# A decoder layer on one NeuronCore: where VectorE leaves the recurrence's state between its scan and the product with C

## The chip, the cores and the metric

One Trainium2 chip, one of its cores (five engines: TensorE or PE, VectorE or DVE, ScalarE or ACT, GpSimd or POOL, and SyncE, which issues the DMAs). The metric is the device time of one execution in microseconds (us); lower is better.

## The reference, cut to what matters

The kernel computes one decoder layer for 64 sequences of 128 tokens with 512 features: a Mamba block, a banded cross attention and a mixture of 8 small experts, each behind a layer norm and added to x. The change is in the Mamba block:

```
proj = einsum('blh,ph->blp', x, in_proj_w);  h_in, gate = split(proj)
u    = silu(conv(h_in) + conv_b)                          # I = 1024 channels
ts, Bm, Cm = split(einsum('bli,pi->blp', uT, x_proj_w))   # N = 16 states
dt   = softplus(einsum('blr,ir->bli', ts, dt_proj_w) + dt_proj_b)
dA   = exp(dt[..., None] * A);   dBx = (dt * uT)[..., None] * Bm[:, :, None, :]
hstates = scan over l of  h = dA * h + dBx
y    = einsum('blin,bln->bli', hstates, Cm) + D * uT
y    = y * silu(gate);   out = einsum('bli,hi->blh', y, out_proj_w)
```

## The kernel before

**Groups.** The 64 sequences go in 32 groups of GB = 2. An iteration g of a software pipeline does the state recurrence of group g ("cur"), the projections, convolution and step sizes of group g + 1 ("nxt"), the output projection and attention of group g - 1 ("p1") and the experts of group g - 2 ("p2"). One iteration from the middle is written twice inside a loop over g; the first three and the last four stand on their own. Every engine has its own list of calls, written out by hand; nothing reorders them, and engines meet through semaphores that count up.

**The 64 steps of a group.** The 1024 channels are 8 blocks `ic` of 128 partitions, the 16 states are 8 pairs `r`; step s = 8 ic + r handles one block and one pair of states: 2 states x 2 sequences x 128 tokens = 512 elements per partition. A step has five parts:

- `decays(g, s)` on ScalarE (lines 452 to 465): two ACTIVATE of 254 elements write exp(delta * a) into PSUM bank s % 2 (`DAR = 2`). Four of the bank's 512 elements, those at token 0 of every state and sequence, are zero and are never written (the memset of line 1392 sets them once), so that the scan starts anew there. It waits for `h_done` of scan s - 2, which read that bank last.
- `times_b(g, s)` on GpSimd (L300): du * B into slot s % 8 of the SBUF ring `ring`. It waits for `hc_used`, which TensorE raises when it has read the slot's last tenant.
- `scan(g, s)` on VectorE (L1454): reads decays from PSUM and the ring slot, writes the states over the ring slot.
- The product with C over the same ring slot: `times_c` on VectorE (L1439) for the 24 steps of `DVE_C` (s % 8 is 1, 4 or 7), on GpSimd (L309) for the other 40. Both read the slot and `bc`, both in SBUF. SyncE may load the next group's `bc` row r once product 56 + r is made.
- `y_sum(g, s)` on TensorE (L1066): transposes of the slots of steps s - 1 and s, added up in PSUM bank 2.

The product and the scan on VectorE as they stand:

```
nc.vector.tensor_tensor(ring[:, s % RING, :], ring[:, s % RING, :],
                        bc[:, s % RS, 2:4, :].rearrange("p a t -> p (a t)"),
                        ALU.mult).then_inc(hcd_done, 1)
nc.vector.tensor_tensor_scan(ring[:, s % RING, :], ps[:, s % DAR, :], ring[:, s % RING, :], 0.0, ...)
```

**What stands between.** VectorE's list also has the softplus (`soft_step`, L1423 to L1434, two SBUF tensors each), the convolution (L1582), the layer norms' statistics, the product with the gate (`y_step`, L1448), the attention's row maxima (L1489), `addq` (L1496), `rden` (L1499), `on` (L1503) and the router. Between `decays`, ScalarE evacuates PSUM banks 3 to 7 for TensorE (copies L526, L551, L561, L566, L596; the attention's exp L592; layer norm L469; step size L489) and loads an activation table (ACT_TABLE_LOAD) when it goes from one function set to another. `attention(.., "wide")` (L600) on ScalarE waits for `rden`, TensorE's L1040 for it, and `on` for that.

## Time and profile before

| | |
|---|---|
| median of 3 runs | 5532.19 us (5530.11 to 5533.7) |
| profiled execution's own time | 5533.42 us |
| its span, first to last instruction | 5531.6 us |
| busy: DVE / PE / POOL / ACT | 90% / 87% / 82% / 73% of the span |
| granted TensorE clock | 0.964 of 2.4 GHz over the span |

Busy is the time in which an engine ran at least one instruction. The idle time of a group of instructions is what the engine stood still just before them, with the instruction that ended it ("releaser"). The chain of waits is followed back from the last instruction: at each step to what released it, or to the instruction before it on its engine; "issue" in it is time in which the engine waited for nothing that the profile shows. Instructions of one engine overlap a little in the timeline: 1.21 us scans follow each other every 1.13 us.

### The profile page before, as it was taken

To read this page: it belongs to the slowest core of one execution; us is meant where nothing else is said; L and a number is where in the kernel's file an instruction comes from. 1 tells how busy PE (TensorE), PEld (TensorE's weight loads), DVE (VectorE), ACT (ScalarE), POOL (GpSimd) and SP (SyncE) were. 2 spreads that over 40 slices of the span, in tenths; PEclk is the share of its full clock that TensorE was granted. 3 is DMA by queue.
4 is the path that set the end of the run, shared out by engine and by line. 5 is a ranking of instruction groups with operands and counts; after the bars stand their busy time and mean duration, and the time that the engine had idled before them with its cause. 6 is when DMAs were issued, how large, how long until landed. Compare 5 with 4: busy or idle time off the path is not lost.

```text
span 5531.6 us, 139169 instructions
## 1 busy us (share of the span) xinstructions
PE 4796.2 (87%) x51012; PEld 3435.7 (62%) x51012; DVE 4955.4 (90%) x7075; ACT 4058.8 (73%) x7812; POOL 4541.5 (82%) x3464
## 2 busy tenths in 40 slices
PE   5788888988888988888989888989888988898876
PEld 3566666666666666666666666666666666666653
DVE  3999999999999999999999999999999999999972
ACT  3677777877777777777877777777777777777752
POOL 2988888888888888888888888888888888888870
PEclk8899999999999999999999999999999999999986
DMA  3211222221212221212221222221212221221100
GB/s 112 71 63 42 70 68 74 70 66 42 74 64 74 70 67 41 74 64 74 71 67 40 74 64 74 74 70 34 77 64 70 74 74 38 70 69 66 62 9 11
DMA packets 114693, 350.19 MB, mean 63 GB/s; under 512 B 13057, under 2 KB 14849, under 8 KB 113921
## 3 DMA queue, kind: packets, MB, share of 16 engines
q1 hardware_dynamic: 114048, 341.51, 19.0%
q8 instruction: 416, 6.82, 0.5%
q14 instruction: 229, 1.87, 0.1%
HBM read 323.64 MB, written 17.83 MB: 62 GB/s over the span
## 4 chain that ended last, share of the span: by engine, by line
PE 46%; DVE 18%; issue 15%; POOL 11%; ACT 7%; DVEq 1%; POOLq 0%; ACTq 0%
POOL ring L300 7%; PE ps L1066 7%; PE ps L1114 6%; DVE ring L1454 5%; PE ps L1096 5%; PE ps L982 4%; PE ps L957 4%; POOL ring L309 4%; PE ps L1134 3%; PE ps L1010 3%; DVE nmax L1489 3%; ACT ps L462 3%; DVE ring L1439 2%; DVE tmp L1423 2%; PE ps L1021 1%
## 5 line engine op out<-in xcount | busy, mean ns | idle before, releaser
L300 POOL TENSOR_TENSOR ring<-du,bc 128x512 f32<-128x512 f32 x2048 | 2741.9, 1356 | 577.7 <-PE ps L1066 352.3
L1454 DVE TENSOR_TENSOR_SCAN ring<-ps,ring 128x512 f32<-128x512 f32 x2048 | 2456.7, 1211 | 201.2 <-POOL ring L300 103.1
L462 ACT ACTIVATE ps<-delta,a_neg 128x254 f32<-128x254 f32 x4096 | 1761.5, 468 | 326.9 <-DVE ring L1454 320.9
L309 POOL TENSOR_TENSOR ring<-ring,bc 128x512 f32<-128x512 f32 x1280 | 1776.5, 1394 | 232.5 <-DVE ring L1454 230.6
L1066 PE MATMUL ps<-ident,ring 128*128 128x128 f32 x8192 | 1103.7, 282 | 73.7 <-DVE ring L1439 43.1
L1066 PEld LDWEIGHTS ps<-ident,ring 128*128 128x128 f32 x8192 | 962.9, 145 | 193.5 <-issue 119.1
L1439 DVE TENSOR_TENSOR ring<-ring,bc 128x512 f32<-128x512 f32 x768 | 755.4, 987 | 3.4
L592 ACT ACTIVATE probs_mem<-ps 128x768 f32<-128x768 f32 (+1 forms) x512 | 455.9, 911 | 176.0 <-PE ps L1010 174.4
L1134 PE MATMUL ps<-w_in,xt_a 128*128 128x256 f32 x2048 | 488.8, 394 | 12.8 <-DVE hc L1582 8.1
L1114 PE MATMUL ps<-xt_a,w_in 128*128 128x256 f32 x2048 | 476.6, 386 | 7.1 <-DVE hc L1582 4.1
L1096 PE MATMUL ps<-w_outp,yz 128*128 128x512 f32 x1024 | 462.5, 599 | 18.7 <-ACT yz L526 18.7
L1489 DVE TENSOR_REDUCE nmax<-ps 128x8 f32<-128x1280 f32 x256 | 380.7, 1487 | 78.4 <-PE ps L982 73.8
L1134 PEld LDWEIGHTS ps<-w_in,xt_a 128*128 128x128 f32 x2048 | 398.1, 200 | 68.4 <-DVE hc L1582 8.9
L1114 PEld LDWEIGHTS ps<-xt_a,w_in 128*128 128x128 f32 x2048 | 381.6, 191 | 76.7 <-issue 17.7
L1582 DVE SCALAR_TENSOR_TENSOR hc<-ps,conv_w,hc 128x254 f32<-128x254 f32 (+2 forms) x768 | 363.1, 473 | 62.2 <-ACT hc L537 42.7
L1096 PEld LDWEIGHTS ps<-w_outp,yz 128*128 128x128 f32 x1024 | 190.1, 191 | 227.9 <-issue 199.8
L982 PE MATMUL ps<-qk 32*32 32x160 f32 (+2 forms) x16384 | 296.2, 297 | 0.0
L1010 PE MATMUL ps<-qk 32*128 32x192 f32 (+1 forms) x4096 | 286.8, 397 | 0.0
L1021 PE MATMUL ps<-probs_mem,v_aug 128*32 128x192 f32 (+1 forms) x4096 | 229.8, 367 | 44.0 <-ACT probs_mem L592 43.9
L579 ACT ACTIVATE qk<-ps,b_qk 128x512 f32<-128x512 f32 x256 | 170.6, 678 | 125.6 <-PE ps L957 125.6
L957 PE MATMUL ps<-xb,w_qk 128*128 128x512 f32 x512 | 241.1, 593 | 2.8 <-ACT qk L579 1.3
L1010 PEld LDWEIGHTS ps<-qk 32*128 32x128 f32 x4096 | 186.3, 197 | 68.4 <-issue 63.1
(136 smaller groups left out, 6362.2 us busy)
## 6 DMA issues: line engine op xcount, KB each, us to landing
w_in<-in_w_in SPq DMA_DIRECT2D x256, 512.0 KB, 3.7
bc<-bc_rows SPq DMA_DIRECT2D x256, 512.0 KB, 4.1
x_new<-in_x SPq DMA_DIRECT2D x32, 512.0 KB, 6.2
x_res<-in_x SPq DMA_DIRECT2D x32, 512.0 KB, 5.5
enc<-in_ctx SPq DMA_DIRECT2D x64, 256.0 KB, 5.3
out<-x_att SPq DMA_DIRECT2D x32, 512.0 KB, 2.8
w_outp<-in_w_outp SPq DMA_DIRECT2D x1, 2048.0 KB, 8.0
bc_rows<-bc_sb SPq DMA_DIRECT2D x32, 32.0 KB, 1.5
```

The lines of the kernel that those rows point to most:

```text
L300: nc.gpsimd.tensor_tensor(ring[:, s % RING, :].rearrange("p (n t) -> p n t", n=2), du[:, q % 2, (ic % 2) * NT:(ic % 2 + 1) * NT].rearrange ...
L309: nc.gpsimd.tensor_tensor(ring[:, s % RING, :], ring[:, s % RING, :], bc[:, s % RS, 2:4, :].rearrange("p a t -> p (a t)"), ALU.mult).then_ ...
L462: nc.scalar.activation(ps[:, s % DAR, (n % 2) * NT:(n % 2 + 1) * NT].rearrange("p (b t) -> p b t", b=GB)[:, :, 1:T], delta[:, ic, :].rearr ...
L982: last = nc.tensor.matmul(ps[32 * a:32 * a + 32, PS_ATT + hp, j * NEAR + lo:j * NEAR + hi], qk[r:r + 32, j, n * P + 32 * a:n * P + 32 * a ...
L1010: last = nc.tensor.matmul(ps[:, PS_ATT + hp, a * WIN + lo:a * WIN + hi], qk[r:r + 32, 2 + j, blk * P:(blk + 1) * P], qk[r:r + 32, j, at:at ...
L1066: last = nc.tensor.matmul(ps[:, PS_Y, b * T:(b + 1) * T], ring[:, t % RING, n * NT + b * T:n * NT + (b + 1) * T], ident[:], start=False, s ...
L1096: last = nc.tensor.matmul(ps[:, PS_ATT + b, :], yz[:, ic, b * T:(b + 1) * T], w_outp[:, ic, :], start=(ic == 0), stop=(ic == NI - 1))
L1114: last = nc.tensor.matmul(ps[:, PS_B, a * NT:(a + 1) * NT], w_in[:, slot, k, a * P:(a + 1) * P], xt_a[:, k, :], start=(k == 0), stop=(k == ...
L1134: last = nc.tensor.matmul(ps[:, PS_B, b * NT:(b + 1) * NT], xt_a[:, k, b * T:(b + 1) * T], w_in[:, slot, k, :], start=(k == 0), stop=(k == ...
L1439: nc.vector.tensor_tensor(ring[:, s % RING, :], ring[:, s % RING, :], bc[:, s % RS, 2:4, :].rearrange("p a t -> p (a t)"), ALU.mult).then_ ...
L1454: nc.vector.tensor_tensor_scan(ring[:, s % RING, :], ps[:, s % DAR, :], ring[:, s % RING, :], 0.0, ALU.mult, ALU.add).then_inc(h_done, 1)
L1489: nc.vector.tensor_reduce(nmax[:, n].rearrange("p j (a r) -> p a j r", r=32)[:, :, :, DH], ps[:, PS_ATT:PS_ATT + 4, 0:NJ * NEAR].rearrange ...
```

## The change

1. For the 24 steps of `DVE_C`, `scan` writes the states over the decays in PSUM bank s % 2, in place of the ring slot. `times_c` on VectorE reads them from there and writes the product to the ring slot.
2. Since the next user of the bank would overwrite states that the product still needs, `decays` of step s + 2 waits for that product (`hcd_done`) where s is in `DVE_C`. The scan has also overwritten the bank's four zeros, so `decays` first copies four zeros from a new SBUF tile `zeros` to their places (one ScalarE COPY of 4 elements).
3. VectorE's list has every `times_c(g, s)` close behind `scan(g, s)` and ahead of `scan(g, s + 2)`. Seventeen of the 24 move forward, product 63 from the next iteration to the end of its own; products 1, 17, 23, 31, 39, 47 and 60 keep their place behind their scan.
4. GpSimd sets `zeros` at the start, and three waits count it.

```diff
@@ decays, ScalarE
+                if (s - DAR) % SG in DVE_C:
+                    reached(act, hcd_done, g * NDC + dvc(s - DAR + 1) if s >= DAR else (g - 1) * NDC + dvc(s - DAR + SG + 1))
+                    nc.scalar.copy(ps[:, s % DAR, :].rearrange("p (k t) -> p k t", t=T)[:, :, 0:1],
+                                   zeros[:].rearrange("p (k o) -> p k o", o=1)).then_inc(da_reset, 1)
                 act.wait_ge(h_done, g * SG + s + 1)
@@ times_c, VectorE
-                nc.vector.tensor_tensor(ring[:, s % RING, :], ring[:, s % RING, :],
+                nc.vector.tensor_tensor(ring[:, s % RING, :], ps[:, s % DAR, :],
@@ scan, VectorE
-                nc.vector.tensor_tensor_scan(ring[:, s % RING, :], ps[:, s % DAR, :], ring[:, s % RING, :], 0.0,
+                state = ps[:, s % DAR, :] if s in DVE_C else ring[:, s % RING, :]
+                nc.vector.tensor_tensor_scan(state, ps[:, s % DAR, :], ring[:, s % RING, :], 0.0,
@@ iteration, VectorE (three of the moves)
                 if cur:
                     scan(g, 36)
+                    times_c(g, 36)
                     scan(g, 37)
...
                     attention(g, 1, "max", 3)
                 if cur:
-                    times_c(g, 36)
                     scan(g, 39)
...
                 if cur:
-                    times_c(g, 55)
                     scan(g, 57)
+                    times_c(g, 57)
                 if p1:
                     attention(g, 1, "rden")
                 if cur:
                     scan(g, 58)
-                    times_c(g, 57)
```

The order of VectorE's instructions late in an iteration, from the layer norm's statistics to `soft_step`, before (scans of 56 and 57 ahead of `rden`, product 55 between them; L1454 is the scan and L1439 the product):

```order
L1408 TENSOR_SCALAR ln_rs_e<-ln_mv_e 128x1
L1438 REGISTER_ALU
L1439 TENSOR_TENSOR ring<-ring,bc 128x512
L1452 REGISTER_ALU
L1454 SCALAR_TENSOR_TENSOR ring<-ps,ring 128x512
L1499 RECIPROCAL rden<-ps 128x32
L1452 ISA
L1454 SCALAR_TENSOR_TENSOR ring<-ps,ring 128x512
L1438 REGISTER_ALU
L1439 TENSOR_TENSOR ring<-ring,bc 128x512
L1503 TENSOR_TENSOR o_sb<-ps,o_sb 128x512 x2
```

Now, the same place (L1463 is the scan, L1447 the product, L1508 `rden`, L1512 `on`):

```order
L1416 TENSOR_SCALAR ln_rs_e<-ln_mv_e 128x1
L1460 REGISTER_ALU
L1463 SCALAR_TENSOR_TENSOR ps<-ps,ring 128x512
L1446 REGISTER_ALU
L1447 TENSOR_TENSOR ring<-ps,bc 128x512
L1508 RECIPROCAL rden<-ps 128x32
L1460 ISA
L1463 SCALAR_TENSOR_TENSOR ring<-ps,ring 128x512
L1512 TENSOR_TENSOR o_sb<-ps,o_sb 128x512 x2
```

Product 57 went from behind scan 58 to ahead of `rden`; product 55 went to behind scan 55.

ScalarE's instructions around the decays of steps 49, 50 and 51, before (the three rows of L462 ACTIVATE; x2 is one step's pair):

```order
L526 COPY yz<-ps 128x256
L462 ACT_TABLE_LOAD
L462 ACTIVATE ps<-delta,a_neg 128x2x127 x2
L460 REGISTER_ALU
L462 ACTIVATE ps<-delta,a_neg 128x2x127 x2
L595 ISA
L596 COPY o_sb<-ps 128x512
```

Now (the decays are L470, the resets L466):

```order
L534 COPY yz<-ps 128x256
L197 REGISTER_ALU
L466 COPY ps<-zeros 128x4
L470 ACT_TABLE_LOAD
L470 ACTIVATE ps<-delta,a_neg 128x2x127 x2
L468 REGISTER_ALU
L470 ACTIVATE ps<-delta,a_neg 128x2x127 x2
L603 ISA
L604 COPY o_sb<-ps 128x512
L197 REGISTER_ALU
L466 COPY ps<-zeros 128x4
```

A reset stands ahead of the decays of step 49 (whose bank step 47 used), and one ahead of those of step 51; the number of table loads is the same.

## Rows read from the trace of the kernel before

**Rows 1.** The page: span, busy time of each engine.
```profile
span 5531.6 us, 139169 instructions
PE 4796.2 (87%) x51012; PEld 3435.7 (62%) x51012; DVE 4955.4 (90%) x7075; ACT 4058.8 (73%) x7812; POOL 4541.5 (82%) x3464
```
**Rows 2.** The chain that ended last, shares by engine.
```profile
PE 46%; DVE 18%; issue 15%; POOL 11%; ACT 7%; DVEq 1%; POOLq 0%; ACTq 0%
```
**Rows 3.** Busy time by stretch, one iteration in five pieces; stretch, length, engines.
```profile
2246.50:2334.30 87.80, 81.19 (x1027) 57.71 (x1028) 81.70 (x131) 61.40 (x122) 76.72 (x61) 0.98 0.12 39
2334.30:2361.90 27.60, 22.61 (x269) 17.89 (x270) 27.29 (x34) 22.70 (x40) 20.81 (x17) 0.94 0.14 40
2361.90:2379.30 17.40, 16.30 (x162) 11.04 (x161) 13.53 (x17) 15.24 (x33) 16.91 (x13) 1.00 0.01 4
2379.30:2401.50 22.20, 18.65 (x100) 13.51 (x99) 21.41 (x28) 18.50 (x34) 17.12 (x13) 1.00 0.53 169
2401.50:2411.50 10.00, 8.97 (x42) 6.06 (x40) 9.91 (x15) 8.52 (x19) 10.00 (x8) 1.00 0.68 240
```
**Rows 4.** Groups by line on VectorE: count, busy, mean ns, idle before.
```profile
L1454 DVE TENSOR_TENSOR_SCAN ring<-ps,ring 128x512 f32<-128x512 f32 x2048 | 2456.7, 1211 | 201.2 <-POOL ring L300 103.1 <-ACT ps L462 94.2 <-issue 0.3
L1439 DVE TENSOR_TENSOR ring<-ring,bc 128x512 f32<-128x512 f32 x768 | 755.4, 987 | 3.4
L1434 DVE TENSOR_TENSOR du<-delta,u 128x512 f32<-128x512 f32 x128 | 89.1, 696 | 0.0
L1496 DVE TENSOR_TENSOR qk<-ps,qk 128x512 f32<-128x512 f32 x128 | 81.8, 679 | 16.2 <-PE ps L992 16.2
```
**Rows 5.** Timeline of VectorE around 2340, 2370, 2382 and 2403 us.
```profile
2339.62 0.68 DVE L1439 TENSOR_TENSOR ring<-ring,bc 128x512 f32<-128x512 f32 x1
2340.22 1.22 DVE L1454 TENSOR_TENSOR_SCAN ring<-ps,ring 128x512 f32<-128x512 f32 x1
2341.47 0.69 DVE L1439 TENSOR_TENSOR ring<-ring,bc 128x512 f32<-128x512 f32 x1
...
2370.49 1.75 DVE L1439 TENSOR_TENSOR ring<-ring,bc 128x512 f32<-128x512 f32 x1
...
2382.64 1.77 DVE L1439 TENSOR_TENSOR ring<-ring,bc 128x512 f32<-128x512 f32 x1
2384.33 1.28 DVE L1503 TENSOR_TENSOR o_sb<-ps,o_sb 128x512 f32<-128x512 f32 x2
...
2402.88 1.28 DVE L1439 TENSOR_TENSOR ring<-ring,bc 128x512 f32<-128x512 f32 x1
...
2405.46 1.62 DVE L1439 TENSOR_TENSOR ring<-ring,bc 128x512 f32<-128x512 f32 x1
```
**Rows 6.** Timeline of GpSimd, the products of 2370 us and after.
```profile
2369.21 1.26 POOL L309 TENSOR_TENSOR ring<-ring,bc 128x512 f32<-128x512 f32 x1
2370.44 2.94 POOL L300 TENSOR_TENSOR ring<-du,bc 128x512 f32<-128x512 f32 x2
```
**Rows 7.** Groups by line on ScalarE: the decays and the smallest ACTIVATE.
```profile
L462 ACT ACTIVATE ps<-delta,a_neg 128x254 f32<-128x254 f32 x4096 | 1761.5, 468 | 326.9 <-DVE ring L1454 320.9
L605 ACT ACTIVATE small<-small 128x16 f32<-128x16 f32 x32 | 6.9, 216 | 132.8 <-DVE small L1538 132.8
```
**Rows 8.** Timeline of ScalarE and TensorE: who is on time for whom.
```profile
2345.64 0.87 ACT L462 ACTIVATE ps<-delta,a_neg 128x254 f32<-128x254 f32 x2 [1.44 <-DVE ring L1454]
...
2378.40 0.88 ACT L462 ACTIVATE ps<-delta,a_neg 128x254 f32<-128x254 f32 x2
...
2382.34 1.09 PE L1040 MATMUL ps<-ident,probs_mem 128*128 128x128 f32 x8
```
**Rows 9.** Who waited for whom: us in total, times, longest.
```profile
POOL ring L300 <- PE ps L1066: 352.3, 229, 4.4
ACT ps L462 <- DVE ring L1454: 320.9, 245, 4.1
```

More of the change, by code:

```diff
@@ L110, in decoder_layer @@
         nmax = sb("nmax", [P, NBLK, NJ, P])
+        zeros = sb("zeros", [P, 2 * GB])
         ln_st = {k: sb("ln_st_" + k, [P, GB, 6]) for k in "ate"}
@@ L279, in _ @@
             nc.gpsimd.memset(neg_half[:], -0.5).then_inc(const_done, 1)
+            nc.gpsimd.memset(zeros[:], 0.0).then_inc(const_done, 1)
             nc.gpsimd.memset(v_aug[:, :, :, DH + 1:32], 0.0).then_inc(att_zero, 1)
@@ L453, in _ @@
             act.wait_ge(da_zeroed, 1)
+            act.wait_ge(const_done, 2)
             def decays(g, s):
@@ L1608, in iteration @@
                     scan(g, 4)
+                    times_c(g, 4)
                     scan(g, 5)
@@ L1624, in iteration @@
                     scan(g, 7)
+                    times_c(g, 7)
                 if p1:
@@ L1636, in iteration @@
                     scan(g, 9)
+                    times_c(g, 9)
                 if nxt:
@@ L1652, in iteration @@
                     scan(g, 12)
+                    times_c(g, 12)
                 if p1:
@@ L1667, in iteration @@
                     scan(g, 15)
+                    times_c(g, 15)
                 if p1:
@@ L1672, in iteration @@
                     scan(g, 16)
-                    times_c(g, 15)
                 if p1:
@@ L1688, in iteration @@
                     scan(g, 20)
+                    times_c(g, 20)
                     scan(g, 21)
@@ L1706, in iteration @@
                     scan(g, 28)
+                    times_c(g, 28)
                 if p1:
@@ L1724, in iteration @@
                     scan(g, 33)
+                    times_c(g, 33)
                     y_step(g, 3)
@@ L1758, in iteration @@
                     soft_step(1, g, 3)
+                    times_c(g, 41)
                     scan(g, 42)
@@ L1763, in iteration @@
                     scan(g, 44)
+                    times_c(g, 44)
                     scan(g, 45)
-                    times_c(g, 41)
                     y_step(g, 4)
@@ L1779, in iteration @@
                     scan(g, 49)
+                    times_c(g, 49)
                     scan(g, 50)
@@ L1829, in iteration @@
                     scan(g, 63)
+                    times_c(g, 63)
                 if nxt:
```

23 lines of the change are left out of this document (6 added, 17 removed).

## The prediction

> **What bounds the kernel now.** The busy shares come first: VectorE 90%, TensorE 87%, GpSimd 82%, ScalarE 73% [rows 1]. With four engines this close no share names the bound, so the chain of waits comes next: 46% of it is TensorE and only 18% VectorE [rows 2]. It also says where. Read over one iteration (the loop repeats every 165.2 us, from scan 0 at 2236.3 us to scan 0 at 2401.5), the chain stays on TensorE almost without a break from its output projection at 2246.5 us to the row maxima at 2334.3, and is on VectorE, GpSimd and ScalarE for the rest. So I cut the iteration into five stretches [rows 3] and price the change in each:
>
> - (a) 87.8 us: TensorE busy 81.2, the chain's own.
> - (b) 27.6 us: VectorE busy 27.3, without a gap.
> - (c) 17.4 us: ScalarE 15.2, GpSimd 16.9, VectorE only 13.5.
> - (d) 22.2 us: VectorE 21.4.
> - (e) 10.0 us: VectorE 9.9, GpSimd 10.0.
>
> **What the change removes.** The product is worth a look. Its mean is 987 ns [rows 4], but single ones take 0.68 and 0.69 us or 1.75 and 1.77 [rows 5]. The one at 2370.49 starts just after a GpSimd product (2370.44) and ends 1.75 us later; that is GpSimd's 1.26 us plus its own time. The pair of GpSimd products takes 2.94 us instead of 2 x 1.26 [rows 6]: the second one waits in turn. So a VectorE instruction with two SBUF tensors and a GpSimd one exclude each other. `addq` reads one tensor from PSUM and one from SBUF: 679 ns [rows 4], although GpSimd is busy 82% of the time. The changed product has its operands, so I give it 0.68. That takes 768 x (0.987 - 0.679) = 237 us from VectorE's busy time (4955 to about 4720), and some 0.45 us from GpSimd at each collision; GpSimd's gain is bounded by zero and by a like 237 us.
>
> The Trainium skill speaks against this price. "VectorE: DVE Perf Modes", section "The TRN2 errata — SBUF-src ops pay a fixed extra latency per instruction", gives a PSUM source a fixed 120 cycles against 58 from SBUF, at 0.96 GHz. By an estimate from that page each changed product would be 65 ns longer than the same one from SBUF, and with three such products on the path of the sum below I would say 6 us more, 5481. The trace doesn't show such a surcharge: 679 ns with PSUM [rows 4] beside 0.68 and 0.69 for undisturbed products from SBUF [rows 5].
>
> **What it adds.**
>
> - 768 resets on ScalarE. No 4-element copy is in the trace; the nearest is an ACTIVATE of 16 elements, 216 ns [rows 7]. Below it is zero, above it the 468 ns of 254 elements. I take 0.15 us of ScalarE's time, since two decays of 468 ns each take only 0.88 as a pair [rows 7, 8] and the overlap of 0.06 is saved once more. That is 24 x 0.15 = 3.6 us an iteration; ScalarE stands at 73%, so most is hidden by its waits, but not where ScalarE runs through.
> - A wait for one's own result. Behind its own scan the product starts 1.25 us after the scan's start (2340.22, 2341.47) [rows 5] and not 1.13: 0.12 more, at the 17 products that newly stand so. 2 us an iteration of VectorE's time.
> - A later release of the bank. The decays of s + 2 wait for the product: at least 0.12 + 0.60, plus the reset. In exchange VectorE itself gets to scan s + 2 later by the same product. From the product's end the chain is reset 0.15, decays 0.88, scan s + 2: 1.03 us, beside scan s + 1 with 1.13. Where ScalarE is free this just fits. What is queued behind the decays (exp of the scores, copies for TensorE) is late by up to 0.87; ScalarE waited for a scan 245 times, 7.7 an iteration, for 320.9 us in all [rows 9], and 24 of 64 banks are concerned. That is the second rival.
> - The scan's output to PSUM. No row has VectorE writing 512 elements there. Bounds: nothing (ScalarE's decays, written to PSUM, are at 468 ns no slower than anything of its size), and one more pass over the elements (third rival). I take nothing.
> - The rest costs nothing: one memset of 16 bytes at the start; product 63 leaves VectorE earlier, so SyncE may issue its load of that `bc` row earlier, and nothing else on its queue moves; `y_sum` finds its slots earlier.
>
> **The sum.** By stretch, for one iteration:
>
> - (a) TensorE's own work; VectorE is lighter by some 4 us here, which TensorE's 81.2 of 87.8 hides: 0.
> - (b) Product 36 stood here behind the row maxima and leaves ahead of them: 0.60 less (2339.62 to 2340.22) [rows 5]. One new wait behind scan 44: 0.12 more. Gain 0.5.
> - (c) The decays of scan 57 come at 2378.40, right behind ScalarE's other work [rows 8]; GpSimd's shorter products meet a ScalarE that isn't faster. One reset on the path: loss 0.15.
> - (d) Product 57 took 1.77 us and `on` started when it ended, at 2384.33 [rows 5]. Now it stands ahead of `rden` and delays it by 0.72. TensorE's L1040, at 2382.34 for 1.09 [rows 8], would end at 2384.15 at the latest, and its first half, which is enough for `on`, earlier. Gain 0.2 to 0.7: 0.5.
> - (e) Products 63 and 1, 1.28 and 1.62 us [rows 5], hold 0.60 and 0.94 of waiting. ScalarE's layer norm and decays follow them closely. All of the first, less than half of the second: 1.0.
>
> Together 1.85 us of 165.2, over 31 iterations 57 us. The profiled execution took 5533.4, so 5476; its time is 1.2 above the median of the three runs, so **5475 us** on their scale, 1.0% faster. A quarter of what VectorE's busy time loses: the rest turns into waiting for TensorE in (a) and for ScalarE in (c).
>
> **The rivals.**
>
> - *VectorE's time was the bound after all.* For it: 90%, and 99% in (b). Then TensorE's share of the chain is only where its order happens to sit, and (a) shrinks too. All of it: 237 less the new waits, 17 x 0.12 x 32 = 65, is 172 us: 5360. Half way up from my sum is 5418. Against: TensorE stands at 87% and would be the bound soon.
> - *ScalarE holds the bank's release against everything behind it* (slower). The decays that start on the scan's end now start 0.87 later. For it: at 2345.64 the decays of step 43 start 1.44 us into a wait for scan 41 [rows 8], and product 41 still stands behind a `soft_step` that reads two SBUF tensors; ScalarE's next copies and exps are TensorE's evacuations. If half of the 7.7 waits an iteration pass 0.87 on, that is 3.35 us, less the 1.85: 1.5 x 31 = 47 slower, 5579. It decides from 2.1 waits an iteration on. Against: 24 of 64 steps give 2.9 of the 7.7, and the 320.9 us of ScalarE's waits are a cushion.
> - *The scan slows when it writes the bank it reads* (slower). If reading and writing took turns, a scan would cost a pass of 512 elements more, some 0.59 us, the spacing of a product: 24 x 0.59 = 14.2 us an iteration, against 7.4 gained on VectorE, 2 lost to the waits. VectorE then has 154 + 8.8 us of work; with half of that on the path 4.4 x 31 = 136 slower, 5668. Against: a scan takes 1211 ns, twice a product, so it has time between elements.
> - *Nothing that can be told.* The locks are gone and each engine waits for the next: 5532.
>
> **How the numbers follow.** About 0.2%, 11 us, is what a measurement can tell from no change. My forecast, 5475 with its own range of 5435 to 5518, has 0.48; the first rival 0.24; no change 0.10; the ScalarE rival 0.13; the slow scan 0.05. Faster by over 0.2%: 0.48 + 0.24 = 0.72. Same 0.10. Slower 0.18. The range reaches from 5385, which leaves out the end of the first rival, to 5560, which takes in a smaller form of the ScalarE rival and leaves out the slow scan.
>
> **What would show each step right or wrong.** The product's mean near 680 ns and not 987; GpSimd's two products down from 1356 and 1394 ns; the scan's mean unchanged at 1211, for both outputs; a new group of 768 copies of 128x4 near 0.2 us; ScalarE's wait for VectorE larger and now partly for the product; VectorE busy near 4720 with more idle time, ended by TensorE and ScalarE; TensorE's share of the chain up. The prediction is wrong if the time falls under 5435 while TensorE's busy stretch (a) gets shorter (first rival), or if scans of the changed steps take longer, or if ScalarE's waits for the product turn up in the chain.

## The result, and the profile after

The changed kernel takes 5580.2 us (median of 4 runs), the kernel before beside it 5532.9: a ratio of 1.0086, interval 1.0074 to 1.0098. It is 47 us slower, where I had forecast 57 faster, and it lies outside my range.

The page of the changed kernel: busy times, then the shares of the chain of waits.

```profile
PE 4852.2 (87%) x51012; PEld 3484.2 (62%) x51012; DVE 4800.1 (86%) x7075; ACT 4129.6 (74%) x8580; POOL 4342.9 (78%) x3465
PE 44%; issue 16%; DVE 15%; ACT 15%; POOL 8%; DVEq 1%; ACTq 0%; POOLq 0%
```

Against [rows 1] VectorE lost 155 us and GpSimd 199, as meant. But TensorE, whose instructions are the same 51012, is busy 56 us longer. In the chain ScalarE went from 7% [rows 2] to 15%.

Groups by line on VectorE, the changed kernel:

```profile
L1463 DVE TENSOR_TENSOR_SCAN ring<-ps,ring 128x512 f32<-128x512 f32 x1280 | 1542.1, 1212 | 55.9 <-POOL ring L302 36.1 <-ACT ps L470 19.2
L1463 DVE TENSOR_TENSOR_SCAN ps<-ps,ring 128x512 f32<-128x512 f32 x768 | 941.0, 1225 | 232.0 <-ACT ps L470 212.8 <-POOL ring L302 14.8 <-issue 1.3
L1447 DVE TENSOR_TENSOR ring<-ps,bc 128x512 f32<-128x512 f32 x768 | 530.0, 690 | 22.1
L1438 DVE TENSOR_TENSOR delta<-delta,lnv 128x512 f32<-128x512 f32 x128 | 131.3, 1026 | 1.1 <-ACT lnv L520 1.1
```

and the `soft_step` instruction of L1438 in the kernel before, where it is L1430:

```profile
L1430 DVE TENSOR_TENSOR delta<-delta,lnv 128x512 f32<-128x512 f32 x128 | 89.2, 697 | 1.1 <-ACT lnv L512 1.1
```

The product fell from 987 ns [rows 4] to 690. The scan that writes the bank takes 1225 ns, the one that writes the ring 1212: 13 ns more. Waiting for decays grew from 94.2 us [rows 4] to 212.8 + 19.2. The `soft_step` instruction, which still has two SBUF tensors, takes 1026 ns instead of 697. Some collisions with GpSimd have only changed their victim.

GpSimd and ScalarE in the changed kernel: two groups by line, then two lines of who waited for whom.

```profile
L302 POOL TENSOR_TENSOR ring<-du,bc 128x512 f32<-128x512 f32 x2048 | 2656.6, 1315 | 716.0 <-PE ps L1074 497.9 <-DVE du L1442 215.3
L466 ACT COPY ps<-zeros 128x4 f32<-128x4 f32 x768 | 126.0, 164 | 235.4 <-DVE ring L1447 234.9
```

```profile
ACT ps L466 <- DVE ring L1447: 234.9, 215, 3.8
ACT ps L470 <- DVE ring L1463: 140.4, 141, 3.6
```

GpSimd's `times_b` is down from 1356 ns to 1315, but it waits 497.9 us for TensorE instead of 352.3 [rows 9]. The reset costs 164 ns. ScalarE waits 234.9 us for products and 140.4 for scans, together 54 more than the 320.9 of [rows 9].

So the prices held and the time did not. Where it went shows when the iterations are taken one by one. Two that follow each other (length, busy times, then mean granted clock, DMA share and GB/s):

```profile
912.93:1082.25 169.32, 152.00 (x1595) 109.31 (x1594) 149.34 (x222) 128.72 (x270) 135.94 (x109) 0.95 0.19 64
1082.25:1247.35 165.10, 147.60 (x1596) 106.50 (x1595) 150.12 (x222) 128.79 (x270) 135.71 (x109) 0.98 0.21 67
```

and one of the kernel before:

```profile
2236.29:2401.50 165.21, 147.59 (x1595) 106.15 (x1594) 154.06 (x222) 126.57 (x245) 141.78 (x109) 0.98 0.20 64
```

Two facts. The long iterations (169.3) have the same instructions as the short ones, TensorE busy 4.4 us longer at a granted clock of 0.95 instead of 0.98. And the short ones (165.1) are no faster than before, although VectorE does 4 us less work. Two theories followed, which the first expectations name: A, TensorE's clock; B, ScalarE's hold on the bank (the second rival of the forecast).

The clock first. Timeline of TensorE in the changed kernel, in a long iteration:

```profile
1365.89 2.78 PE L1074 MATMUL ps<-ident,ring 128*128 128x128 f32 x24
1368.61 1.72 PE L1029 MATMUL ps<-probs_mem,v_aug 128*32 128x192 f32 x32
...
1373.41 6.74 PE L1151 MATMUL ps<-u,w_xt 128*128 128x256 f32 x16 [2.71 <-ACT yz L534]
```

and its stretches there:

```profile
1366.00:1373.00 7.00, 4.70 (x59) 3.58 (x57) 6.82 (x11) 6.97 (x13) 5.24 (x5) 0.98 0.14 54
1373.00:1379.40 6.40, 5.99 (x14) 4.83 (x15) 3.91 (x5) 4.77 (x12) 5.18 (x5) 0.50 0.02 4
```

The same place in the kernel before:

```profile
2356.99 1.09 PE L1066 MATMUL ps<-ident,ring 128*128 128x128 f32 x8 [1.02 <-DVE ring L1439]
2358.01 1.72 PE L1021 MATMUL ps<-probs_mem,v_aug 128*32 128x192 f32 x32
...
2361.35 3.72 PE L1143 MATMUL ps<-u,w_xt 128*128 128x256 f32 x16 [1.25 <-ACT yz L526]
```

Before, TensorE waited twice here, 1.02 us for product 44 and 1.25 for ScalarE's `yz`. In the changed kernel product 44 comes early, the 24 transposes of the sum of y run through, and one wait of 2.71 us is left. Behind it the granted clock is 0.50, the level of 1.2 GHz, and the projection to `ts` takes 6.74 us instead of 3.72. TensorE did not lose work; it got ahead of it, stood still in one piece, and came back at half speed.

It does not come back so each time. The same projection in another iteration of the changed kernel, behind a wait that is hardly shorter:

```profile
1207.07 3.71 PE L1151 MATMUL ps<-u,w_xt 128*128 128x256 f32 x16 [2.61 <-ACT yz L534]
```

I counted the 24 iterations in the middle, numbers 4 to 27. All have a wait of 2.5 to 2.7 us here, and the clock fell behind it in 14. At the start of an iteration it fell in 14 too. The kernel before has a wait of 1.1 to 1.6 us ahead of `ts` in its 24, and no fall at either place. At two further places, 51 to 54 and 101 to 105 us into an iteration, the clock falls in both kernels, in most iterations. Over the whole span it stood at 0.50 for 540 us in the changed kernel and for 397 us in the one before.

### The profile page after: what moved, and what is told of

It is laid out like the page before. It is cut to its first block, busy times and chain, and to the rows that moved or that the text cites. A ratio compares the mean times of both kernels' runs of the same rounds, so it can differ in the third digit from the quotient of the medians.

```text
span 5575.2 us, 140890 instructions
## 1 busy us (share of the span) xinstructions
PE 4852.2 (87%) x51012; PEld 3484.2 (62%) x51012; DVE 4800.1 (86%) x7075; ACT 4129.6 (74%) x8580; POOL 4342.9 (78%) x3465
## 4 chain that ended last, share of the span: by engine, by line
PE 44%; issue 16%; DVE 15%; ACT 15%; POOL 8%; DVEq 1%; ACTq 0%; POOLq 0%
PE ps L1074 6%; POOL ring L302 5%; PE ps L1122 5%; PE ps L1104 5%; ACT ps L470 5%; PE ps L990 4%; DVE ps L1463 4%; DVE ring L1463 4%; PE ps L965 3%; PE ps L1018 3%; PE ps L1151 3%; POOL ring L311 3%; DVE nmax L1498 2%; ACT probs_mem L600 2%; PE ps L1157 2%
## 5 line engine op out<-in xcount | busy, mean ns | idle before, releaser
L302 POOL TENSOR_TENSOR ring<-du,bc 128x512 f32<-128x512 f32 x2048 | 2656.6, 1315 | 716.0 <-PE ps L1074 497.9
L311 POOL TENSOR_TENSOR ring<-ring,bc 128x512 f32<-128x512 f32 x1280 | 1663.2, 1306 | 286.0 <-DVE ring L1463 281.6
L470 ACT ACTIVATE ps<-delta,a_neg 128x254 f32<-128x254 f32 x4096 | 1761.4, 467 | 142.8 <-DVE ring L1463 140.4
L1463 DVE TENSOR_TENSOR_SCAN ring<-ps,ring 128x512 f32<-128x512 f32 x1280 | 1542.1, 1212 | 55.9 <-POOL ring L302 36.1
L1463 DVE TENSOR_TENSOR_SCAN ps<-ps,ring 128x512 f32<-128x512 f32 x768 | 941.0, 1225 | 232.0 <-ACT ps L470 212.8
L1074 PE MATMUL ps<-ident,ring 128*128 128x128 f32 x8192 | 1121.9, 286 | 11.9 <-POOL ring L311 7.2
L1074 PEld LDWEIGHTS ps<-ident,ring 128*128 128x128 f32 x8192 | 985.2, 148 | 116.6 <-issue 73.5
L1447 DVE TENSOR_TENSOR ring<-ps,bc 128x512 f32<-128x512 f32 x768 | 530.0, 690 | 22.1
L466 ACT COPY ps<-zeros 128x4 f32<-128x4 f32 x768 | 126.0, 164 | 235.4 <-DVE ring L1447 234.9
L1095 PE MATMUL ps<-ident,yg 128*128 128x128 f32 x512 | 106.4, 290 | 183.8 <-issue 125.1
```

Source lines behind the costliest of these rows:

```text
L302: nc.gpsimd.tensor_tensor(ring[:, s % RING, :].rearrange("p (n t) -> p n t", n=2), du[:, q % 2, (ic % 2) * NT:(ic % 2 + 1) * NT].rearrange ...
L311: nc.gpsimd.tensor_tensor(ring[:, s % RING, :], ring[:, s % RING, :], bc[:, s % RS, 2:4, :].rearrange("p a t -> p (a t)"), ALU.mult).then_ ...
L470: nc.scalar.activation(ps[:, s % DAR, (n % 2) * NT:(n % 2 + 1) * NT].rearrange("p (b t) -> p b t", b=GB)[:, :, 1:T], delta[:, ic, :].rearr ...
L1074: last = nc.tensor.matmul(ps[:, PS_Y, b * T:(b + 1) * T], ring[:, t % RING, n * NT + b * T:n * NT + (b + 1) * T], ident[:], start=False, s ...
L1447: nc.vector.tensor_tensor(ring[:, s % RING, :], ps[:, s % DAR, :], bc[:, s % RS, 2:4, :].rearrange("p a t -> p (a t)"), ALU.mult).then_inc ...
L1463: nc.vector.tensor_tensor_scan(state, ps[:, s % DAR, :], ring[:, s % RING, :], 0.0, ALU.mult, ALU.add).then_inc(h_done, 1)
```

## Experiments

"Before" in this part is the kernel before, run beside on the same chip: 5532.7 to 5535.6 us in the five batches. Ratios are to that kernel; where kernels of two batches are compared by their times, these 3 us are the doubt.

### The order without the PSUM operand

```diff
-                nc.vector.tensor_tensor(ring[:, s % RING, :], ps[:, s % DAR, :],
+                nc.vector.tensor_tensor(ring[:, s % RING, :], ring[:, s % RING, :],
...
-                state = ps[:, s % DAR, :] if s in DVE_C else ring[:, s % RING, :]
+                state = ring[:, s % RING, :]
```

The wait and the reset in `decays` are gone too; what stays is the place of each product.

> The kernel before with VectorE's products moved as in the change, scan and product still over the ring slot, no reset and no new wait of ScalarE. Theory A (TensorE's clock: product 44 leaves y_sum, TensorE's two short waits around it become one of 2.6 us ahead of the ts projection, the granted clock falls behind it and the projection's 3.7 us become up to 6.7): this kernel shows the same fall, some iterations of 167 to 169 us, time 5550 to 5590. Theory B (ScalarE holds the release of the bank and what is queued behind it): without that wait the loss is gone, 5500 to 5535, every iteration near 165.

Measured: 5807.5 us, ratio 1.0502 (1.0485 to 1.0520). Both theories missed this by over 200 us, and it tests neither: its waits ahead of `ts` are at most 1.4 us, with no fall behind them, and its clock falls at other places. Groups by line on VectorE:

```profile
L1442 DVE TENSOR_TENSOR ring<-ring,bc 128x512 f32<-128x512 f32 x768 | 937.0, 1220 | 22.1
```

The change is the difference of two large numbers: the moves alone cost 274 us, and the PSUM operand in the moved places is worth 227. A product right behind its scan meets GpSimd more often (mean 1220 ns, not 987): in the order before, more of the products stand clear of GpSimd.

### Without the resets

```diff
-                    nc.scalar.copy(ps[:, s % DAR, :].rearrange("p (k t) -> p k t", t=T)[:, :, 0:1],
-                                   zeros[:].rearrange("p (k o) -> p k o", o=1)).then_inc(da_reset, 1)
```

The wait for the product (`hcd_done`) stands in the same branch and stays: ScalarE still waits 228.8 us for products in this kernel's trace, beside 234.9 in the changed kernel. Without the resets the scan starts from other values than the reference's.

> The changed kernel without the 768 resets (the four zeros are left as the scan made them, so the recurrence of two tokens later steps starts from other values); the wait for the product stays. Theory A: time within 0.3% of the changed kernel unless the phase of the clock's falls shifts, 5565 to 5590. Theory B: 24 x 0.1 to 0.16 us an iteration come off ScalarE's path, 5500 to 5560.

Measured: 5577.3 us, ratio 1.0082 (1.0065 to 1.0099), 3 us under the changed kernel, within the intervals, as theory A had it. The 768 resets are not what costs. What the wait for the product costs is not told by this run, and no run takes it out alone.

### Keeping TensorE busy where it waits

`fill(bank, n)` issues n transposes of a tile of zeros that accumulate into a bank whose sum is under way. They add nothing to it and wait for nothing.

```diff
+            def fill(bank, n):
+                for _ in range(n):
+                    nc.tensor.matmul(ps[:, bank, 0:P], zfill[:], ident[:], start=False, stop=False,
+                                     is_transpose=True, skip_group_check=True)
...
                 if p1:
+                    fill(PS_ATT, 8)
                     y_turn(g - 1, 7, cur)
...
                     y_turn(g, 4, nxt)
+                    fill(PS_Y, 16)
                 if nxt:
                     ts_in(j, cur)
```

> The changed kernel with 16 transposes of a zero tile added into the open sum of bank 2 just ahead of the ts projection, and 8 into the open output projection ahead of the last turn of y, where TensorE only waits (1.7 and 0.9 us of work in gaps of 2.6 and 1.1 us); adding zeros changes no value. Theory A: the falls at 9 and 125 us into an iteration vanish, all iterations near 165, time 5500 to 5530. Theory B: nothing gained, 5575 to 5590.

Measured: 5528.9 us, ratio 0.9992 (0.9982 to 1.0001). More work on the busiest engine, and 51 us less; in the 24 middle iterations no fall is left at either place. The same in the kernel before (8 transposes, ahead of `ts` alone):

> The kernel before with 8 transposes of a zero tile ahead of the ts projection (0.9 us in a gap of 1.25 us). Both theories: within 0.2% of before, 5525 to 5545, since no fall of the clock stands there; it says whether the filler itself costs or gains anything.

Measured: 5529.3 us, ratio 0.9993 (0.9984 to 1.0003). Theory A stands: the change adds falls of the clock at two places, and with them it loses the 51 us, a little more than the whole 47 by which it is slower. It also leaves the change with nothing gained: 5529 us with both places filled, 5529 the kernel before with `ts` filled. Each place alone:

> The changed kernel with only the 16 zero transposes ahead of the projection to ts. Theory A (TensorE's clock, two falls that the changed kernel adds: one at this projection, one at the start of an iteration): this one is the longer (6.8 us at the lower level), so more than half of the 51 us that both fillings gave back comes from it: 5535 to 5555 us. If the two falls follow from each other (a late projection makes the next iteration's first wait), this one alone gives all of it: 5529 to 5535. Theory B (the filling helps by something else than the clock, for instance by delaying TensorE's load of weights): no reason for this place, 5560 to 5580.

Measured: 5532.7 us, ratio 1.0002 (0.9993 to 1.0012).

> The changed kernel with only the 8 zero transposes ahead of the turn of y's last piece (y_turn 7). Theory A: the shorter of the two falls (3.4 us at the lower level, some 1.7 us longer), every second iteration: 15.5 x 1.7 = 26 us back, 5550 to 5565. If this fall is only a consequence of the other: 5572 to 5585. Theory B: as good as the other filling.

Measured: 5547.9 us, ratio 1.0027 (1.0017 to 1.0037). One gives back 48 us, the other 32, both 51: the two are not independent. The time that TensorE's clock stood at 0.50 in the whole span goes the same way: 540 us in the changed kernel, 465 with `y_turn` 7 filled, 421 with `ts` filled, 407 with both, 397 in the kernel before. The filling of one place also changes how often the clock falls at the others, so the prices of the single falls can't be read from these runs.

An attempt to get the two waits of before back without filling is to leave product 44 as it was:

```diff
+    DVE_PS = [1, 4, 7, 9, 12, 15, 17, 20, 23, 25, 28, 31, 33, 36, 39, 41, 47, 49, 52, 55, 57, 60, 63]
...
                     scan(g, 44)
-                    times_c(g, 44)
                     scan(g, 45)
...
+                    times_c(g, 44)
                     soft_step(4, g, 3)
```

> The changed kernel with product 44 alone as before: its operands from the ring and its place behind scan 46. TensorE then has its two short waits around the sum of y as before, instead of one of 2.6 us ahead of ts. Theory A: the fall of the clock at ts goes without any filling, 5535 to 5558 us, and its iterations no longer alternate between 165 and 169 us. Theory B (the clock is a companion, the time is lost where VectorE and ScalarE wait for each other): one product of 24 changes 1/24 of it: 5575 to 5585.

Measured: 5560.3 us, ratio 1.0051 (1.0035 to 1.0068), just above theory A's range. One of 24 products is worth 20 us, far more than its share, but less than the filling, and the two waits did not come back: ahead of `ts` TensorE waits 1.9 us in 17 of the 24 iterations, and the clock stays, and 2.3 us in 7, and it falls in each. Over the span it stood at 0.50 for 526 us.

### The form on the products that collide

For the steps named, scan, product and decays take the changed form; all others are as before. Three products move:

```diff
+    DVE_PS = [1, 23, 49, 57, 63]
...
-                if p1:
-                    times_c(g - 1, 63)
...
                     scan(g, 49)
+                    times_c(g, 49)
...
                     scan(g, 57)
+                    times_c(g, 57)
...
                     scan(g, 63)
+                    times_c(g, 63)
```

> The kernel before with the changed form (scan leaves its states in the bank, reset of four zeros) for the steps 1, 23, 49, 57 and 63 alone, whose products took 1.62, 1.76, 1.76, 1.77 and 1.29 us; 49, 57 and 63 follow their scan at once; the other 19 keep ring and place. Theory C (a product that stood clear of GpSimd had nothing to gain, and its move is what costs): these five hold 0.93 + 1.07 + 1.07 + 1.08 + 0.60 = 4.75 us an iteration of VectorE's 7.2 and only 5 resets and 3 moves; a quarter to a third of it is on the path: 5480 to 5510 us. Theory D (TensorE is the bound whatever VectorE saves): 5525 to 5540. If the clock falls as in the whole change, because 57 and 63 do it: 5550 to 5580.

Measured: 5531.3 us, ratio 0.9986 (0.9961 to 1.0011), but eight executions spread from 5503 to 5551. The median is in theory D's range, the best three executions in theory C's, so this run alone decides nothing. In its trace stand a run of iterations of 163.8 us and others of up to 167:

```profile
1246.55:1410.34 163.79, 145.91 (x1595) 105.23 (x1594) 151.99 (x222) 127.01 (x251) 140.08 (x109) 0.99 0.21 66
```

The order of the work and the clock had to be taken apart, so all further kernels but one are filled. The next four have filling at every place where the clock had fallen in any kernel: 8 transposes ahead of `y_turn` 7, 12 between the score transposes "st" 0 and 1 of block 0, 8 and 6 around `y_turn` 3, 16 ahead of `ts`.

> The kernel before with zero transposes at all four places at which the records of any kernel so far show TensorE's granted clock at half (9, 51, 101 and 125 us into an iteration): 8, 12, 8 + 6 and 16 of them. Its iterations last 164.1 us where the clock fell once and 165.2 to 165.9 where it fell for 6.8 us. Theory A (the clock's time is lost on the path): no falls, 31 x 1.5 to 2 us less, 5465 to 5490 us. If the work put in delays TensorE as much as the clock gives: 5525 to 5540.

Measured: 5553.1 us, ratio 1.0032 (1.0021 to 1.0043), slower than either expectation.

> The changed kernel with the same filling at all four places, so that both kernels run at the full clock. Theory A1 (the change gains what the forecast said, 1.85 us an iteration, and the clock took it): 50 to 60 us under the filled kernel before, 5410 to 5440. Theory A2 (the change gains nothing on the path, the clock only made it slower than before): within 15 us of the filled kernel before. Theory B (later decays cost): 20 us or more above it.

Measured: 5508.8 us, ratio 0.9948 (0.9934 to 0.9961).

> The changed form for the steps 1, 23, 49, 57 and 63 alone, with the filling at all four places. Its undisturbed iterations lasted 163.8 us with one fall of 3.4 us left. Theory C (the five locked products are the whole gain): 1 us an iteration under the filled kernel before, so 25 to 45 us less than it, and at or under the changed kernel with the filling. Theory D (TensorE bounds both): the same as the filled kernel before within 10 us.

Measured: 5528.6 us, ratio 0.9987 (0.9978 to 0.9996).

> The changed form for the steps 1, 57 and 63 alone, the three products on which the terms (d) and (e) of the forecast rest (0.5 and 1.0 us an iteration), with the filling at all four places. If these terms are right, it lies 1.5 x 31 = 46 us under the filled kernel before; if only the lock of product 63 and 1 counts, 20 to 35; if neither is on the path at the full clock, within 10.

Measured: 5557.3 us, ratio 1.0038 (1.0025 to 1.0052).

The 44 us between the first two (5553.1 and 5508.8) look like theory A1, though both times lie above its ranges. They are not a fair difference: the kernel before has no gap ahead of `y_turn` 7, so eight transposes stand in its way there. They also move its products against GpSimd's. The last of the four says little on the terms (d) and (e): in 5 of its 24 iterations the clock still fell at the start, and while product 57 fell from 1.77 to 0.69 us, product 60, which has its operands in SBUF here, rose from 0.68 to 1.77 (means of the 24). That collision had only moved on. Timeline of VectorE in the filled kernel before, the product of step 39, and of GpSimd beside it:

```profile
2346.65 1.22 DVE L1468 TENSOR_TENSOR_SCAN ring<-ps,ring 128x512 f32<-128x512 f32 x1
2347.90 1.73 DVE L1453 TENSOR_TENSOR ring<-ring,bc 128x512 f32<-128x512 f32 x1
```

```profile
2347.81 1.28 POOL L302 TENSOR_TENSOR ring<-du,bc 128x512 f32<-128x512 f32 x1 [3.04 <-PE ps L1073]
```

GpSimd started 0.09 us earlier and the product takes 1.73 us. (The Trainium skill, "SBUF — State Buffer", section "SBUF: two separate sides", says that whichever of the two starts first holds the shared ports for its whole instruction. The rows agree.) In the kernel before, step 39's product took 0.82 us in the mean of the 24 iterations, here 1.72. GpSimd's start, which waits for TensorE, decides it.

### With filling that fits

> The kernel before with the filling only where its own clock falls (51 and 101 us into an iteration) and 8 transposes ahead of ts: nothing at the start of an iteration, where it has no gap and eight of them stood 0.8 us in the way. Theory A1 (the change gains 1 us or more an iteration at the full clock): this kernel stays 30 us or more above the changed one with its filling (5509), so 5538 or more. Theory A2 (it gains nothing at the full clock): 5495 to 5520; its iterations with one fall lasted 164.1 us, 1.4 to 1.7 of it the fall's.

Measured: 5519.0 us, ratio 0.9976 (0.9966 to 0.9986). This is in A2's range: the filling is worth 14 us to the kernel before, and with each its filling the whole change is about 10 us ahead (5508.8 against 5519.0), not 57. Even these 10 are not clean. Product 39 collides in this filled kernel too, in the mean of the 24 iterations at 1.72 us:

```profile
2335.59 1.73 DVE L1452 TENSOR_TENSOR ring<-ring,bc 128x512 f32<-128x512 f32 x1
```

```profile
2335.50 1.28 POOL L302 TENSOR_TENSOR ring<-du,bc 128x512 f32<-128x512 f32 x1 [3.04 <-PE ps L1073]
```

So the filling gives the kernel before the full clock and takes some of it back, and how much the change itself gains or loses at the full clock stays open by about what this collision costs.

> The changed form for 1, 23, 49, 57 and 63 alone and filling, with 10 instead of 16 transposes ahead of ts (16 ended 0.16 us after the wait they stood in). If that filler delayed it: 5515 to 5525 instead of 5529. If the loss sits at product 39, which collides with GpSimd once its neighbours have shifted: still 5526 to 5532.

Measured: 5508.9 us, ratio 0.9959 (0.9945 to 0.9973). Six transposes fewer ahead of `ts`: 20 us, more than expected.

> The same with step 39 in the changed form too; it stands right behind its scan already, so nothing moves. Product 39 took 1.73 us where the filled kernel collides there and scan 40 was 1.0 us late. If this loss is on the path: 25 to 35 us less than the kernel with five steps. If the next product takes the collision over: the same within 8.

Measured: 5489.8 us, ratio 0.9922 (0.9908 to 0.9936). One step more in the changed form, which moves nothing: 19 us less, between the two expectations. In the kernel with five steps product 39 took 1.72 us, here 0.69; so this is also the nearest price of the collision in the filled kernel before, and it is more than the 10 us above.

> The changed form for all steps whose product stood right behind its scan already (1, 17, 23, 31, 39, 47, 60) and for 49, 57, 63: ten steps, three moves. Theory C (the form pays where it needs no move): the fastest so far, under 5500 us and at or below the kernel with six. If the later release of the bank costs at the four new steps (17, 31, 47, 60): 5 to 20 us above the kernel with six.

Measured: 5466.4 us, ratio 0.9879 (0.9863 to 0.9894). The ten steps beat all 24 by 42 us.

> The kernel before with the changed form for 1, 17, 23, 31, 39, 47, 49, 57, 60 and 63, without any filling. With filling it took 5466 us; the filling was worth 14 us to the kernel before (5519 against 5533) and 71 to the changed one (5509 against 5580). Theory C with the clock as a second, separate effect: 5480 to 5530, faster than before, less steady than the filled kernels. If the clock falls at four places as in the whole change and costs as much: 5530 to 5540.

Measured: 5504.3 us, ratio 0.9941 (0.9928 to 0.9955): without any filling, 29 us faster than before and 76 than the changed kernel. Theory C's range holds this time.

What do the other 14 steps lose, then? The start of some scans, in us behind scan 0 of their iteration, in one iteration of each kernel at a granted clock of 1.00 (the medians of the 24 differ by 0.05 at most):

| kernel | scan 5 | scan 38 | scan 49 | scan 57 | next scan 0 |
|---|---|---|---|---|---|
| before, its own filling | 10.11 | 98.09 | 126.51 | 142.48 | 164.84 |
| change, filled | 9.07 | 97.74 | 126.08 | 141.98 | 164.44 |
| ten steps, filled | 8.48 | 96.99 | 124.92 | 140.73 | 163.20 |
| all but 41, 44, 52, filled | 9.07 | 97.84 | 124.17 | 140.07 | 162.54 |

Three of these iterations as the profile has them (length, busy times, granted clock of 1.00, DMA share, GB/s): before with its own filling,

```profile
2231.47:2396.31 164.84, 149.05 (x1630) 107.50 (x1628) 154.77 (x222) 126.31 (x245) 142.14 (x109) 1.00 0.20 66
```

the change, filled,

```profile
2224.71:2389.15 164.44, 150.36 (x1645) 109.21 (x1644) 150.16 (x222) 128.58 (x270) 136.10 (x109) 1.00 0.20 66
```

and all but three, filled:

```profile
2201.05:2363.59 162.54, 149.58 (x1639) 108.49 (x1638) 149.97 (x222) 128.50 (x267) 136.52 (x109) 1.00 0.20 67
```

VectorE has 4.6 us less to do in the second than in the first, and the iteration is 0.4 shorter; between the second and the third it has the same to do, and 1.9 us go. The last row is the last experiment. From the first three: the whole change is 0.75 us behind the ten steps at scan 38 and takes another 0.41 from there to scan 49 (28.34 against 27.93). In that stretch stand products 41 and 44.

```diff
-                    times_c(g, 41)
                     scan(g, 42)
...
                     scan(g, 44)
-                    times_c(g, 44)
                     scan(g, 45)
+                    times_c(g, 41)
                     y_step(g, 4)
```

(44 and 52 likewise go back to their old places, and all three to ring operands.)

> The changed kernel with filling at all four places (10 transposes ahead of ts), but steps 41, 44 and 52 as before: ring operands, their places behind scan 45, 46 and 54. Theory E (ScalarE's decays of step 43 wait for product 41 behind a softplus step, and those of 46 and 54 likewise, so scans 43 and 49 are late): the 1.24 us an iteration come back, 5509 - 38 = 5460 to 5480 us. Theory F (each of the 14 further moves costs a little): 5500 to 5515 less an eighth, so 5495 to 5510.

Measured: 5446.7 us, ratio 0.9841 (0.9828 to 0.9855), below even theory E's range: three steps of 24 cost 62 us at the full clock (5508.8 against 5446.7). This kernel also has ten transposes ahead of `ts` and not sixteen. In the filled change the sixteen end 0.97 us before what TensorE waits for there, so they take nothing; in this kernel ten just fit, and it has no such wait. It is the fastest kernel of the study, 1.6% under the kernel before.

By the table the whole difference, 1.91 us an iteration, stands between scans 38 and 49 (28.34 against 26.33). From scan 49 to 57, where product 52 is, both take 15.90. So it is 41 and 44 that cost, and 52 is not shown to. How they do it can be read. VectorE in the filled change, from scan 41 on:

```profile
2330.79 1.22 DVE L1477 TENSOR_TENSOR_SCAN ps<-ps,ring 128x512 f32<-128x512 f32 x1
2331.92 0.73 DVE L1445 SCALAR_TENSOR_TENSOR tmp<-tmp,soft 128x512 f32<-128x512 f32 x1
2332.58 0.68 DVE L1461 TENSOR_TENSOR ring<-ps,bc 128x512 f32<-128x512 f32 x1
2333.18 1.21 DVE L1477 TENSOR_TENSOR_SCAN ring<-ps,ring 128x512 f32<-128x512 f32 x1
2334.31 1.70 DVE L1448 SCALAR_TENSOR_TENSOR delta<-delta,tmp 128x512 f32<-128x512 f32 x1
2335.93 1.21 DVE L1477 TENSOR_TENSOR_SCAN ring<-ps,ring 128x512 f32<-128x512 f32 x1
...
2351.03 1.23 DVE L1477 TENSOR_TENSOR_SCAN ps<-ps,ring 128x512 f32<-128x512 f32 x1 [2.46 <-ACT ps L472]
```

and ScalarE beside it:

```profile
2333.29 0.17 ACT L468 COPY ps<-zeros 128x4 f32<-128x4 f32 x1 [2.69 <-DVE ring L1461]
2333.39 0.87 ACT L472 ACTIVATE ps<-delta,a_neg 128x254 f32<-128x254 f32 x2
...
2337.17 0.87 ACT L472 ACTIVATE ps<-delta,a_neg 128x254 f32<-128x254 f32 x2 [0.93 <-DVE ring L1477]
...
2339.62 0.17 ACT L468 COPY ps<-zeros 128x4 f32<-128x4 f32 x1 [0.24 <-DVE ring L1461]
```

Without the three steps, VectorE:

```profile
2307.23 1.21 DVE L1479 TENSOR_TENSOR_SCAN ring<-ps,ring 128x512 f32<-128x512 f32 x1
2308.36 0.72 DVE L1446 SCALAR_TENSOR_TENSOR tmp<-tmp,soft 128x512 f32<-128x512 f32 x1
2309.01 1.21 DVE L1479 TENSOR_TENSOR_SCAN ring<-ps,ring 128x512 f32<-128x512 f32 x1
2310.14 0.66 DVE L1449 SCALAR_TENSOR_TENSOR delta<-delta,tmp 128x512 f32<-128x512 f32 x1
2310.72 1.21 DVE L1479 TENSOR_TENSOR_SCAN ring<-ps,ring 128x512 f32<-128x512 f32 x1
...
2325.46 1.23 DVE L1479 TENSOR_TENSOR_SCAN ps<-ps,ring 128x512 f32<-128x512 f32 x1 [1.55 <-ACT ps L473]
```

and ScalarE:

```profile
2308.48 0.87 ACT L473 ACTIVATE ps<-delta,a_neg 128x254 f32<-128x254 f32 x2 [1.44 <-DVE ring L1479]
```

From scan 41 to scan 43 it is 5.14 us against 3.49. 0.60 is product 41, which stands in between now. 1.04 is the next `soft_step`, which the 0.60 pushed behind a GpSimd instruction: 1.70 instead of 0.66. ScalarE's decays of step 43 are later too (a wait of 2.69 us and not 1.44), as theory E has it, but they are not what makes scan 43 late: they end at 2334.26, and VectorE is busy with the `soft_step` until 2335.93. The late scan 43 then holds ScalarE. The decays of step 45 wait 0.93 us for it, those of step 46 another 0.24 us for product 44, and behind them ScalarE runs without a gap up to the decays of step 49, for which scan 49 waits 2.46 us instead of 1.55. So theory E named the right steps, and its cause, the wait for the product, has a small part; most comes by VectorE's own order. TensorE, which takes ScalarE's exp and copies, waits in the filled change as well,

```profile
2339.53 0.44 PE L959 MATMUL ps<-band,ident_bf 32*32 32x512 bf16 x16 [0.98 <-ACT probs_mem L602]
...
2348.88 0.69 PE L1158 MATMUL ps<-u,w_xt 128*128 128x256 f32 x2 [0.97 <-ACT yz L536]
```

where without the three steps it runs on:

```profile
2314.36 0.43 PE L960 MATMUL ps<-band,ident_bf 32*32 32x512 bf16 x16
```

## Why the prediction was wrong, point by point

**The prices: right.** The product took 690 ns (0.68 forecast), VectorE's busy time 4800 us (about 4720; 20 of the missing 80 are in the four `soft_step` lines, 486 us instead of 466, where instructions collide that did not before), the reset 164 ns (0.15), the scan into the bank 13 ns more (nothing), GpSimd's products 1315 and 1306 ns. The page of the Trainium skill that I weighed against my rows ("VectorE: DVE Perf Modes", the section on the errata) would have given 65 ns more for a PSUM source; 690 ns, beside 0.68 and 0.69 [rows 5] for undisturbed products from SBUF, shows about 10.

**"The rest costs nothing: ... `y_sum` finds its slots earlier": the step that failed first.** I priced an early product as harmless at worst. It joined two of TensorE's waits into one, and in 14 of 24 iterations the clock fell behind it, and as often at the start of an iteration. Transposes in these two gaps give back 51 us, which is more than the whole loss of 47, and the same in the kernel before gives 4, within its interval. The evidence that a sum for this kernel needs the clock lay in my own rows: the granted clock of stretch (b) was 0.94 [rows 3], and no term spoke of it. Why the clock falls behind one wait of 2.6 us and not behind another stays open. And this step explains the loss, not the missing gain; that is in the next two.

**Stretch (b), "gain 0.5": wrong by the most.** I took product 36 out of (b) and charged one new wait of 0.12. But product 41 is moved inside it too, between a `soft_step` and scan 42, and I named it only under the second rival. At the full clock (b), scan 38 to 49, shrank by 0.08 (28.42 to 28.34); without 41, 44 and 52 it is 26.33, so 2.09 shorter. Part of that is the collision of product 39, which stands in the 28.42 alone: with five steps, taking it away shortened scan 38 to 49 by 0.54. The rest was there to be had, and the moves of 41 and 44 took all of it. (c), "loss 0.15", from scan 49 to 57, came out 0.07 shorter.

**(d) and (e), "0.5" and "1.0": partly there, and (a), "0": wrong.** From scan 0 to 5 the change is 1.04 us shorter, as (e) says. From scan 57 to 63 it is 1.75 shorter, more than the 0.5 of (d). But from scan 63 to the next scan 0 it is 1.86 longer, so of both terms 0.94 is left of 1.5. Product 63 is 0.60 of the 1.86. The rest is the `soft_step` behind it, which it pushed into a GpSimd instruction. VectorE, then GpSimd, in the filled change:

```profile
2387.70 1.78 DVE L1452 TENSOR_TENSOR delta<-delta,lnv 128x512 f32<-128x512 f32 x1
```

```profile
2387.66 1.27 POOL L304 TENSOR_TENSOR ring<-du,bc 128x512 f32<-128x512 f32 x1
```

and the same `soft_step` in the kernel before with its own filling:

```profile
2395.98 0.67 DVE L1443 TENSOR_TENSOR delta<-delta,lnv 128x512 f32<-128x512 f32 x1
```

It is so in every one of the 24 iterations, filled or not. Each of the faster kernels moves product 63 as well, so what this costs in the end is not shown.

(a), scan 5 to 38, became 0.69 longer, and TensorE's timeline in the filled change shows where:

```profile
2283.07 0.43 PE L1074 MATMUL ps<-ident,skip 128*128 128x128 f32 x2 [0.33 <-DVE yg L1470]
...
2311.76 0.32 PE L943 MATMUL ps<-band,ident 32*128 32x320 bf16 x4 [0.31 <-DVE x_att L1536]
```

It waits for `y_step` 1 and for the sum x2 of the attention, and products 20 and 33 were moved ahead of just these two. With ten steps, where 20 and 33 stay, neither wait is in the trace, and scan 38 keeps 1.10 of the gain, and not 0.35. Counted from TensorE's output projection to scan 38, it is 88.15 us in the filled kernel before, 88.98 in the change and 88.19 with ten steps (means of the 24). "TensorE's own work" had been a stretch without slack on VectorE's side either.

**The rivals.** VectorE's time as the bound: no; with 4.6 us less of its work an iteration the change gained 0.4 at the full clock. The scan that slows: no, 13 ns. The second rival forecast 5579, and 5580 came, but the number agrees by chance. It had ScalarE late by 0.87 at half of its 7.7 waits, spread over the iteration. In fact three steps cost 2.0 us an iteration at the full clock (62 / 31), two of them by the table, and mostly by VectorE's order and a collision; a wait of 0.24 us for product 44 is what the path shows of ScalarE's hold. The clock, which no rival had, makes the loss. The rival's evidence, product 41 behind a `soft_step`, was the right place to look; I gave it 0.13.

The filling at all places is worth 71 us to the change (5580 to 5509). How far these and the 62 of the three steps overlap was not taken apart: no kernel without the three steps ran unfilled, and in the unfilled change the collision behind scan 42 stands in some iterations and not in others (scan 42 to 43 takes 1.71 to 2.76 us). Nor is it shown why the ten steps and the 21 differ as they do at each scan.

## What to carry to other kernels

Cost a moved instruction by what stands directly behind it in its new place, one by one, and not only by what leaves the old one: products 41 and 63 each pushed a `soft_step` of 0.66 us into a GpSimd instruction, and three steps of 24 took back 62 of the 72 us that the other 21 were worth at the full clock (5519 to 5447; part of the 72 is a collision that the filling made in the kernel before). When TensorE is near its bound, look at how its waits are spread before and after, since one long wait can cost more than two short ones; a few transposes of zeros in the gap, no more than fit it, tell in one run whether the clock is at fault; look in the trace whether they have also shifted a collision. And in a kernel tuned around collisions of VectorE and GpSimd, give the collision-free operands first to the products that need no move.

## What the runs showed of the hardware

- TensorE's granted clock fell to 0.50 (1.2 GHz) ahead of the same projection behind 14 of 24 waits of 2.5 to 2.7 us in the changed kernel and behind all 7 waits of 2.3 us with product 44 as before. It stayed at 1.00 behind the other 10, behind 17 waits of 1.9 us, and behind the 24 waits of 1.1 to 1.6 us of the kernel before. So the length of that one wait does not decide it alone.
- Six to sixteen transposes of zeros in such waits kept the clock at 1.00 in the steady iterations. TensorE then does more work (4894 us busy, not 4852) in a shorter time (5509 us, not 5580). Where they don't fit the wait they cost: six surplus transposes ahead of `ts` were worth 20 us in the kernel with five steps.
- Whether a VectorE product of two SBUF tensors takes 0.68 or 1.73 us is decided by where GpSimd's start falls, and filling on TensorE moves that: the product of step 39 took 0.82 us in the mean of the kernel before and 1.72 with filling.
- VectorE can leave a scan's states in the bank from which it reads its decays, at 1225 instead of 1212 ns for 512 elements, and a product with that PSUM source takes 690 ns in the mean of 768, with GpSimd busy 78% of the span.
